# Last combine stage: first expert's rows and the residual summed by TensorE in PSUM, with diagonal weights from ScalarE

## What is computed

```python
def _L1_ffn_ref(hidden_states, ...):
    ...
    hidden_after_attn = hidden_states + proj_out
    ln2_out = _layernorm(hidden_after_attn, ln2_weight, ln2_bias)
    x = ln2_out.reshape(-1, H)
    logits = jnp.einsum('th,eh->te', x, router_weight)
    gate = jax.nn.softmax(logits, axis=-1)
    top_probs, top_idx = jax.lax.top_k(gate, TOP_K)       # TOP_K = 2
    ...
    moe_out = jnp.einsum('eth,et->th', expert_out, weights).reshape(S, B, H)
    return hidden_after_attn + moe_out
...
x = x + _layernorm(_L1_ffn_ref(_layernorm(x, axis=-1), ...), axis=-1)
return x
```

## Time and profile before

| | us |
|---|---|
| median of 3 runs | 2456.47 |
| lowest and highest run | 2455.84, 2463.76 |
| profiled execution, its time | 2460.9 |
| profiled execution, its span | 2459.2 |
| last stage, first DMA issue to the end of the span | 65.6 (2393.6 to 2459.2) |
| VectorE busy in the span | 1678.1 (68%) |
| TensorE busy in the span | 1911.8 (78%) |
| ScalarE busy in the span | 1184.7 (48%) |

### The profile page before, as it was taken

How to read it: one execution, slowest core, us unless ns; L and a number is a source line. 1 busy time by engine, 2 the same in 40 slices (tenths; PEclk the granted TensorE clock), 3 DMA queues, 4 the chain that set the end, 5 groups by cost and what they waited for, 6 DMA issues and landing times. The chain is left out here.

```text
span 2459.2 us, 35798 instructions
## 1 busy us (share of the span) xinstructions
PE 1911.8 (78%) x10252; PEld 1465.2 (60%) x10253; DVE 1678.1 (68%) x3193; ACT 1184.7 (48%) x2021; POOL 1515.8 (62%) x1152
## 2 busy tenths in 40 slices
PE   6787879686979787875599999907877784799970
PEld 2445455554555454544499999904655664699970
DVE  1779898989989898985644444437634897644438
ACT  2677777777777767773232222226632441111112
POOL 1799999999999999994133333335622420355532
PEclk9888979798989888887699999958988896799995
DMA  3111111111101011112411111142000014122226
GB/s 123 38 35 40 39 37 36 39 39 37 39 23 52 27 49 31 43 36 77 165 48 47 47 48 48 41 139 77 9 18 11 9 35 163 42 71 70 70 65 192
DMA packets 76780, 138.63 MB, mean 56 GB/s; under 512 B 10369, under 2 KB 47873, under 8 KB 75858
## 3 DMA queue, kind: packets, MB, share of 16 engines
q1 hardware_dynamic: 62994, 99.67, 12.4%
q0 software_dynamic: 13632, 37.24, 4.8%
HBM read 104.86 MB, written 32.01 MB: 56 GB/s over the span
## 5 line engine op out<-in xcount | busy, mean ns | idle before, releaser
L787 DVE TENSOR_TENSOR_SCAN a_hs<-a_dA,a_carry,a_hs 128x512 f32<-128x512 f32 x512 | 628.3, 1264 | 63.5 <-ACT a_dA L559 53.7
L399 POOL TENSOR_TENSOR a_hs<-a_u,a_b_bc 128x1024 f32<-128x1024 f32 (+1 forms) x292 | 634.9, 2182 | 2.3 <-POOL a_u L381 1.9
L929 PE MATMUL a_h_ps<-k_ident,a_hs 128*128 128x128 f32 x2064 | 328.3, 308 | 174.7 <-DVE a_acc L750 95.6
L929 PEld LDWEIGHTS a_h_ps<-k_ident,a_hs 128*128 128x128 f32 x2064 | 268.4, 158 | 293.5 <-DVE a_hs L787 86.2
L559 ACT ACTIVATE a_dA<-a_delta,a_a_neg 128x512 f32<-128x512 f32 x512 | 350.1, 687 | 39.6 <-DVE a_hs L787 38.4
L411 POOL TENSOR_TENSOR a_acc<-a_acc,a_part 128x512 f32<-128x512 f32 x242 | 331.7, 1371 | 28.6 <-ACT a_part L573 28.3
L573 ACT ACTIVATE a_part<-a_h_ps,a_c_tok 128x512 f32<-128x512 f32 x242 | 166.0, 686 | 203.8 <-PE a_h_ps L929 176.0
L1229 POOL DMA_INDIRECT expert_rows<-m0e_ys,k_pair x71 | 78.7, 1109 | 232.5 <-DVE m0e_ys L1285 221.6
L750 DVE SCALAR_TENSOR_TENSOR a_acc<-a_h_ps,a_c_tok,a_acc 128x512 f32<-128x512 f32 x242 | 176.3, 728 | 46.5 <-PE a_h_ps L929 46.4
L863 PE MATMUL a_fx<-a_hT,a_w_x 128*128 128x512 f32 x432 | 200.9, 597 | 2.2 <-ACT a_halo L495 1.4
L1295 DVE TENSOR_TENSOR m0e_hT<-m0e_gs,m0e_u 128x512 f32<-128x512 f32 x70 | 48.2, 688 | 191.5 <-ACT m0e_gs L1248 191.5
(11 more groups left out here) (420 smaller groups left out, 3793.2 us busy)
## 6 DMA issues: line engine op xcount, KB each, us to landing
a_b_bc<-b_rows SPq DMA_DIRECT2D x132, 256.0 KB, 3.2
c_y<-expert_rows SPq DMA_DIRECT2D x16, 512.0 KB, 5.6
q_y<-expert_rows SPq DMA_DIRECT2D x16, 512.0 KB, 5.9
norm_rows<-a_x SPq DMA_DIRECT2D x9, 512.0 KB, 3.3
m0w_up<-in_m_up SPq DMA_DIRECT2D x1, 4096.0 KB, 12.1
m0w_gate<-in_m_gate SPq DMA_DIRECT2D x1, 4096.0 KB, 22.2
m0w_down<-in_m_down SPq DMA_DIRECT2D x1, 4096.0 KB, 32.1
c_xl<-in_L_attn_x SPq DMA_DIRECT2D x8, 512.0 KB, 3.7
```

Of the source, the lines that this page charges most:

```text
L399: last = pool.tensor_tensor(hs[k][:, w, :], u[s][:, w, :], b_bc[:, k:k + 1, :].broadcast_to([P, width, T]), ALU.mult)
L787: dve.tensor_tensor_scan(hs[k][:, c, :], dA[c][:], hs[k][:, c, :], carry[:, hf, c, n:n + 1], ALU.mult, ALU.add).then_inc(s_scan, 1)
L929: last = pe.transpose(hT_ps[j % 2][:, c * P:(c + 1) * P], hs[(n - 1) % NBUF][:, c, j * P:(j + 1) * P], ident[:])
```

## The change

TensorE gets a stream in the phase. For each tile of a unit it issues two fp32 matmuls into one PSUM region of `first[u % 2]`: identity times the hidden rows (start of the sum), and a diagonal matrix with w1 on its diagonal times row1 (end of the sum). ScalarE makes the four diagonals of a unit, `weight[u % 2]`, from the identity with an activation whose scale is w1. VectorE's first four scalar_tensor_tensor are gone; its remaining four take the sum from PSUM in place of the SBUF tile. Two semaphores are new: `s_w` (diagonals made) and `s_f` (a unit's sums done, raised once, by the last of its eight matmuls). The branches for `x_in` and for `store is None`, which this only call never took, are removed too, with the tile `xl`.

The core of the diff:

```diff
-def combine_phase(nc, io, per, tag, x, x_in=None, store=None):
+def combine_phase(nc, io, per, tag, x, store):
...
+    HALF = TJ // 2
...
-        res = Residual(m, per, x, again=store is None)
+        res = Residual(m, per, x, again=False)
         y = [m.sb(f"y{k}", [P, 2, TJ, D]) for k in range(NBUF)]
-        xl = [m.sb(f"xl{k}", [P, TJ, D]) for k in range(2)]
+        weight = [m.sb(f"weight{k}", [P, TJ, P]) for k in range(2)]
         pad = m.sb("pad", [P, 8])
+        first = [[m.ps(f"first{k}{h}", [P, HALF, D]) for h in range(2)] for k in range(2)]
         s_g = [m.sem(f"rows_loaded{k}") for k in range(NBUF)]
+        s_w = m.sem("weights_on_diagonal")
+        s_f = m.sem("first_expert_summed")
...
         @block.scalar
         def _(act):
+            def diagonals(u):
+
+                if u >= 2:
+                    act.wait_ge(s_f, u - 1)
+                for q in range(TJ):
+                    last = act.activation(weight[u % 2][:, q, :], per.ident[:], ACT.Copy, scale=per.top[:, u * TJ + q, 0:1])
+                last.then_inc(s_w, 1)
+
+            diagonals(0)
+            diagonals(1)
             for u in range(NU):
+                if 2 <= u + 1 < NU:
+                    diagonals(u + 1)
                 res.scale(act, (0, u, None), u % 2)
+
+        @block.tensor
+        def _(pe):
+            for u in range(NU):
+                if u >= 2:
+                    pe.wait_ge(s_r, (u - 1) * TJ)
+                for q in range(TJ):
+                    ps = first[u % 2][q // HALF][:, q % HALF, :]
+                    pe.matmul(ps, per.ident[:], per.H[:, u * TJ + q, :], start=True, stop=False)
+                    if q == 0:
+                        pe.wait_ge(s_w, u + 1)
+                        pe.wait_ge(s_g[u % NBUF], 32 * (u // NBUF + 1))
+                    last = pe.matmul(ps, weight[u % 2][:, q, :], y[u % NBUF][:, 0, q, :], start=False, stop=True)
+                last.then_inc(s_f, 1)
 
         @block.vector
         def _(dve):
...
             for u in range(NU):
                 b = u % NBUF
                 dve.wait_ge(s_g[b], 32 * (u // NBUF + 1))
+                dve.wait_ge(s_f, u + 1)
                 for q in range(TJ):
-                    j = u * TJ + q
-                    last = dve.scalar_tensor_tensor(out=y[b][:, 0, q, :], in0=y[b][:, 0, q, :], scalar=per.top[:, j, 0:1],
-                                                    in1=per.H[:, j, :], op0=ALU.mult, op1=ALU.add)
-                link(last)
-                for q in range(TJ):
-                    j = u * TJ + q
-                    dve.scalar_tensor_tensor(out=res.r[u % 2][:, q, :], in0=y[b][:, 1, q, :], scalar=per.top[:, j, 1:2],
-                                             in1=y[b][:, 0, q, :], op0=ALU.mult, op1=ALU.add).then_inc(s_r, 1)
+                    dve.scalar_tensor_tensor(out=res.r[u % 2][:, q, :], in0=y[b][:, 1, q, :], scalar=per.top[:, u * TJ + q, 1:2],
+                                             in1=first[u % 2][q // HALF][:, q % HALF, :], op0=ALU.mult, op1=ALU.add).then_inc(s_r, 1)
                 dve.wait_ge(s_r, (u + 1) * TJ)
                 res.stats(dve, link, (0, u, None), u % 2)
                 if u:
-                    add(u - 1)
-            add(NU - 1)
+                    res.add(dve, link, (0, u - 1, None), (u - 1) % 2, (u - 1) * TJ)
+            res.add(dve, link, (0, NU - 1, None), (NU - 1) % 2, (NU - 1) * TJ)
```

More of the change, by code:

```diff
@@ L1439, in final @@
             pool.tensor_tensor(self.per.RS2[:, bass.ds(t0, TJ)], self.v2[s][:, 1, :], self.half[:], ALU.pow)
-def combine_phase(nc, io, per, tag, x, x_in=None, store=None):
+def combine_phase(nc, io, per, tag, x, store):
     NBUF = 3
     NU = TILES // TJ
+    HALF = TJ // 2
     with ExitStack() as ctx:
         m = Mem(nc, ctx, tag, per.sems)
-        res = Residual(m, per, x, again=store is None)
+        res = Residual(m, per, x, again=False)
         y = [m.sb(f"y{k}", [P, 2, TJ, D]) for k in range(NBUF)]
-        xl = [m.sb(f"xl{k}", [P, TJ, D]) for k in range(2)]
+        weight = [m.sb(f"weight{k}", [P, TJ, P]) for k in range(2)]
         pad = m.sb("pad", [P, 8])
+        first = [[m.ps(f"first{k}{h}", [P, HALF, D]) for h in range(2)] for k in range(2)]
         s_g = [m.sem(f"rows_loaded{k}") for k in range(NBUF)]
+        s_w = m.sem("weights_on_diagonal")
+        s_f = m.sem("first_expert_summed")
         s_r = m.sem("row_used")
-        s_xl = [m.sem(f"x_loaded{k}") for k in range(2)]
         s_o = m.sem("stored")
@@ L1469, in load @@
                     sp.dma_start(y[u % NBUF][:, k], yv[:, k, u * TJ:(u + 1) * TJ, :]).then_inc(s_g[u % NBUF], 16)
[L1470 to L1473, removed]
             def put(u):
-                if store is not None:
-                    sp.wait_ge(res.s_x, u + 1)
-                    sp.dma_start(store[:, u * TJ:(u + 1) * TJ, :], x[:, u * TJ:(u + 1) * TJ, :]).then_inc(s_o, 16)
+                sp.wait_ge(res.s_x, u + 1)
+                sp.dma_start(store[:, u * TJ:(u + 1) * TJ, :], x[:, u * TJ:(u + 1) * TJ, :]).then_inc(s_o, 16)
             for u in range(NU):
@@ L1486, in _ @@
                 put(u)
-            if store is not None:
-                sp.wait_ge(s_o, 16 * NU)
+            sp.wait_ge(s_o, 16 * NU)
         @block.gpsimd
@@ L1509, in _ @@
             link = Link(dve, s_d, 0, pad)
[L1511 to L1514, removed]
             for u in range(NU):
```

## The result

| | before | changed |
|---|---|---|
| median, us | 2459.69 (11 runs) | 2467.48 (11 runs) |
| lowest and highest, us | 2454.40, 2463.76 | 2462.58, 2471.44 |
| ratio to before | 1 | 1.0033, 95% interval 1.0022 to 1.0043 |
| last stage, first DMA issue to the last mark, us | 56.4 | 63.2 |

A forecast was written before the change was run, and what follows sets the result against it. VectorE was taken to bound the last stage. Eighth mark at 2436.7 + 4 S, with S = 5.5: 2458.7 against 2450.04, 8.7 us later; less the product's savings, 8.1 slower: 2464.6 against median 2456.47, range 2455.0 to 2470.0.

The forecast's parts named there:

- last mark: Last stage: start of the last unit's L1392, VectorE's last short statistics instruction; at 2450.04 before, forecast 8.7 us later before a correction.
- The removed part: Last stage, VectorE: the four instructions of L1521 go, 1.70 us a unit, leaving 4.97 of 6.67 us.
- The loop: Last stage: mark, scaling, diagonals two units on, matmuls, VectorE's part; 9.86 + S for two units, against 13.35 us before.
- Its constant part: The loop without S: scaling 4.76, diagonals 1.26, VectorE's part 3.64, hand-overs 0.2; 9.86 us for two units.
- S: TensorE's seven matmuls behind a unit's diagonals: 3.2 us at high clock, 5.9 at low, taken as 5.5 in units 0, 2, 4, 6.
- The clock: TensorE in the last stage: cold at the start of each pair of units after some 5 us idle, warm in the second.
- rival A: TensorE's clock stays up in the last stage, S = 3.2: 2455.4 us, no change; chance 0.20.
- The product: GpSimd's product after its power: 0.20 instead of 0.43 us where VectorE idles, 0.2 us less in each of three loops.
- rival C: Power leaves the addition's shadow at high clock; three loops lose 0.85 us each, stage 3.1 us shorter, 2453.4; chance 0.06.
- The PSUM operand: VectorE's four remaining scalar_tensor_tensor read PSUM: taken at no change, between 0.02 us less and 0.1 us more for one.
- Costed at nothing: Last stage: first two units' diagonals, row loads needed some 10 us after issue, the link behind L1521, SyncE's queue order.
- B: TensorE's clock never rises in the last stage, S = 5.9 throughout: 12.1 us later than before, 2468.5; chance 0.12.

The follow-up runs named there:

- the kernel one unit ahead: Changed kernel with a third weight tile, ScalarE making the diagonals of unit u + 2 ahead of the scaling of unit u: 2456.58 us, ratio 0.9996 to before.

## Why the prediction was right

The forecast was 8.1 us slower, 2464.6 against the median of 2456.47. Measured are 7.8 us between the medians, 0.33%, with an interval of 5.4 to 10.6 us, and 6.8 us in the stage of the profile. The time itself, 2467.48, is 2.9 us above the forecast, because before's median stood 3.2 us higher in these runs. The mechanism came as told; that the total is so close is in part luck, as the terms below show.

- *The removed part.* Where nothing waits, marks stand 5.03 us apart (2421.96 - 2416.93), against 4.97 in the prediction.
- *The loop.* Confirmed from both sides: one place earlier for the diagonals takes 10.3 us off (loop and low clock together), four more of them for each unit put 4.2 us on, 3.5 us of that in the loop's constant part. VectorE waits for sums in units 0, 2, 4 and 6 and in no other.
- *Its constant part.* From mark to mark of units 2 and 4 pass 14.16 us, of which 4.78 are the matmuls with their hand-over: 9.4 is left where I had 9.86 - 0.2, and again 9.4 from unit 4 to unit 6. The diagonals begin 0.1 us before the scaling's last row ends (2406.91 against 2404.93 + 2.07), so one hand-over was counted and doesn't exist; another 0.1 us stands here in the 4.78.
- *S.* I took 5.5 us for each of the four. From the first weighted matmul to VectorE's start pass 5.3, 5.1, 4.8 and 6.2 us, 5.3 in the mean with a hand-over of about 0.1 in it. The forecast's own span, 5.0 to 5.9, misses the 4.8 and the 6.2, and the mean came near by their balance: how long TensorE stays low differs from run to run of matmuls (2.7 us from 2422.69 on, over 5 from 2436.86 on).
- *The clock.* It fell after each idle time of 4.8 to 5.6 us and rose on the way, as forecast. That it costs about 2 us for each of the four sums is shown by the kernel that keeps TensorE busy; rival A was right in its sum (no change if the clock stays up) and wrong in its condition.
- *GpSimd.* The product fell to 0.20 us as forecast, but not for the reason given: in the loops VectorE doesn't idle beside it. That was luck. The power beside the addition stayed at 1.91 to 1.95, so rival C's gain didn't come.
- *The PSUM operand.* Taken at no change; 476 ns against 481. The upper end of the forecast's span held 1.3 us for it, which no run shows. The Trainium skill (VectorE: DVE Perf Modes, the section on the TRN2 errata) has a fixed surplus for a PSUM source, 0.26 us for four by an estimate from that page. It doesn't show here: four take 1.66 us against 1.67.
- *Costed at nothing.* The loads were hidden in the changed kernel, but only because the loop was slow: in the kernel one unit ahead, that cover was gone, and the fourth buffer then took 4.1 us off (52.9 to 48.8). My 10 us of lead for the loads held for the changed kernel (9 to 14 us from the issue of a load to TensorE's use of it, units 4 to 7), not for the faster one. The addition that they stand behind is four units back, not three.
- *Sums that don't hold as written.* The 0.2 us for the product was taken off three times, but the first of the three loops was counted from the first unit's 3.91 us, which has the short product in it already: 0.4 us in all, so the forecast should have read 8.3. In the same way C's 0.85 us could be gained in two loops and not in three, which makes it 2.2 us faster instead of 3.1. B's 12.1 us leave the product's 0.6 us out.

The four sums took 21.4 us instead of 22.0 and the constant parts of the three loops 27.4 instead of 28.1; the start and the last period were 0.1 us longer together. That is the 1.3 us by which the stage came out below the forecast (6.8 instead of 8.1). The change did take 1.7 us per unit from the bound engine. It gave them back as waits, since the work that it added stands on a path that leads over four engines and closes on itself every two units.

## What to carry over

When work is moved from the busiest engine to idle ones, don't add up busy time; write down the loop from one release to the next, with every instruction that stands ahead in each in-order queue, and divide by the units it spans. If that loop is longer than the engine's own work, the order in a queue that is half idle decides: here one place forward, with one more buffer each for diagonals and rows, turned 0.33% slower into about 0.3% faster. And when one bound goes, ask what was hidden behind it; here it was the loads behind three buffers.

## What the runs showed of the hardware

GpSimd's short product on L1403 took 0.43 us in the steady part before, where VectorE ran L1521 beside it, and takes 0.20 us throughout the changed kernel, also where L1532 with its PSUM operand runs beside it (at 2419.16, L1532 from 2418.33 to 2419.99). I had put this down to VectorE idling; it holds in the units where VectorE doesn't idle. The row of before's first unit fits less well: 0.25 us (2406.11), with L1521 beside it until 2406.30. The power on L1401 didn't change: 1.91 us beside L1416 in both kernels. What kind of VectorE operand slows GpSimd was not tried apart.

TensorE's granted clock had fallen behind idle times of 4.8 to 5.6 us in the changed kernel, behind 3.5 and 3.4 us in the kernel one unit ahead, and once behind 1.95 us, in the kernel with the first unit on VectorE. Behind idle times of 0.8 to 1.4 us, in the kernel with four buffers, it stood at 1.00 each time.
